# A two-layer decoder kernel: causal attention masked on its diagonal blocks, with a further contraction row for the masked blocks and buffers cleared one by one

## The reference, cut to what matters

```
scores = jnp.einsum('bhid,bhjd->bhij', q, k) * scale
causal_mask = jnp.triu(jnp.full((Ll, Ll), -10000.0, dtype=scores.dtype), 1)
attn = jax.nn.softmax(scores + causal_mask, axis=-1)
y_softmax = jnp.einsum('bhij,bhjd->bhid', attn, v)
```

## Time and profile before

| | us |
|---|---|
| median of 3 runs | 6885.89 |
| lowest and highest | 6875.44, 6894.77 |
| the profiled execution, its own time | 6882.64 |
| its span, first to last instruction | 6880.8 |
| TensorE's mean granted clock over the span | 0.874 of full speed |
| PE, PEld, DVE, ACT, POOL busy | 5450.3, 2943.8, 4755.6, 3102.1, 2124.6 |

### The profile page before, as it was taken

How to read it: one execution, slowest core, us unless ns; L and a number is a source line. 1 busy time by engine, 2 the same in 40 slices (tenths; PEclk the granted TensorE clock), 3 DMA queues, 4 the chain that set the end, 5 groups by cost and what they waited for, 6 DMA issues and landing times. The chain is left out here.

```text
span 6880.8 us, 138736 instructions
## 1 busy us (share of the span) xinstructions
PE 5450.3 (79%) x46679; PEld 2943.8 (43%) x46679; DVE 4755.6 (69%) x8810; ACT 3102.1 (45%) x4684; POOL 2124.6 (31%) x2727
## 2 busy tenths in 40 slices
PE   3686657688888846978498999996567799999659
PEld 2343335222222223434356888885535233333234
DVE  5464675899999954456656777763555899999644
ACT  0233434477777722224433444442224577777512
POOL 0100325577777730004026555541306000000000
PEclk6898978799999978989796888886778899999879
DMA  2220007222222210002243443431108222222100
GB/s 63 47 45 16 6 14 258 68 58 58 59 59 59 57 32 20 0 0 106 103 143 113 115 119 114 121 98 63 56 16 270 62 64 64 65 65 64 53 12 12
DMA packets 747524, 484.29 MB, mean 70 GB/s; under 512 B 516504, under 2 KB 682240, under 8 KB 741568
## 3 DMA queue, kind: packets, MB, share of 16 engines
q1 hardware_dynamic: 747200, 480.04, 24.5%
HBM read 282.34 MB, written 196.37 MB: 70 GB/s over the span
## 5 line engine op out<-in xcount | busy, mean ns | idle before, releaser
L1504 ACT ACTIVATE c0a_raised<-c0a_sb 128x1024 f32<-128x1024 f32 (+1 forms) x832 | 836.3, 1025 | 317.3 <-PE c0a_sb L1316 313.0
L1269 POOL TENSOR_SCALAR c0a_prob<-c0a_raised 128x1024 f32<-128x1024 f32 (+1 forms) x832 | 864.7, 1039 | 366.7 <-ACT c0a_raised L1504 335.7
L1504 ACT ACTIVATE c1a_prob<-c1a_sb 128x1024 f32<-128x1024 f32 (+1 forms) x832 | 828.5, 1029 | 206.6 <-PE c1a_sb L1316 202.9
L1392 DVE TENSOR_REDUCE c1a_pmax<-c1a_sa 128x2 f32<-128x802 f32 (+1 forms) x704 | 698.2, 992 | 68.2 <-PE c1a_sa L1284 64.2
L1392 DVE TENSOR_REDUCE c0a_pmax<-c0a_sa 128x2 f32<-128x802 f32 (+1 forms) x704 | 697.1, 990 | 55.2 <-PE c0a_sa L1284 51.1
L1284 PE MATMUL c0a_sa<-c0a_K,c0a_Q 48*128 48x401 bf16 (+1 forms) x2048 | 471.8, 349 | 181.7 <-DVE c0a_pmax L1392 107.7
L1284 PE MATMUL c1a_sa<-c1a_K,c1a_Q 48*128 48x401 bf16 (+1 forms) x2048 | 466.2, 346 | 103.9 <-DVE c1a_pmax L1392 49.1
L1335 PE MATMUL c0a_pv<-c0a_prob,c0a_V 128*9 128x256 f32 x6656 | 524.9, 386 | 4.7 <-POOL c0a_prob L1269 4.1
L1335 PE MATMUL c1a_pv<-c1a_prob,c1a_V 128*9 128x256 f32 x6656 | 519.4, 383 | 0.7 <-issue 0.5
L1284 PEld LDWEIGHTS c0a_sa<-c0a_K,c0a_Q 48*128 48x128 bf16 x2048 | 129.1, 93 | 667.7 <-DVE c0a_pmax L1392 340.4
L3020 PE MATMUL dd_lb<-dd_src 64*128 64x128 f32 (+1 forms) x3584 | 357.2, 345 | 38.9 <-DVE dd_AB L3211 15.7
(11 more groups left out here) (606 smaller groups left out, 11199.4 us busy)
## 6 DMA issues: line engine op xcount, KB each, us to landing
dd_src<-unit_in SPq DMA_DIRECT2D x32, 1024.0 KB, 7.8
k_ctx<-c0k_parts SPq DMA_DIRECT2D x16, 1200.8 KB, 6.1
c0a_K<-k_ctx SPq DMA_DIRECT2D x128, 150.1 KB
k_ctx<-c1k_parts SPq DMA_DIRECT2D x16, 1200.8 KB, 5.9
c1a_K<-k_ctx SPq DMA_DIRECT2D x128, 150.1 KB
unit_in<-ds_raw SPq DMA_DIRECT2D x32, 512.0 KB, 2.6
unit_v<-ds_vs SPq DMA_DIRECT2D x32, 512.0 KB, 2.6
unit_in<-dp_res SPq DMA_DIRECT2D x32, 512.0 KB, 2.9
```

Of the source, the lines that this page charges most:

```text
L1269: pool.tensor_scalar(prob[0:r, in_ring(v, c), :, :, :], raised[0:r, in_ring(v, c), :, :, :], 1.0, math.exp(-FLOOR), ALU.min, ALU.max).then ...
L1392: dve.tensor_reduce(pmax[:, u, :, 2 * pr + s, k], sa2[:, :, 0:w], AX.X, ALU.max).then_inc(a_reduced, 1)
L1504: act.activation(dst[0:r, in_ring(v, c), :, :, :], sb_[0:r, in_both(v, c), :, :, :], ACT.Exp).then_inc(b_exp, 1)
```

## The change

It touches four things in `attention_stage`:

- The mask of pass A is now one triangle `above` of 128 x 128, read twice, and written to quarters 0 and 3 of the piece (256 columns instead of 512). The mask of pass B is one triangle `below`, again read twice by each of its two matmuls, and written only to the 128 queries on the diagonal of the key tile (256 columns instead of 512).
- The block that is masked whole gets its -10000 from contraction row 64 (`FULL`): `K` holds 125 there for keys 128 to 255, `Q` holds -80 for queries 0 to 127. `K` is zero instead of one in rows 0 to 95.
- DVE clears and fills the buffers of `K` and row 64 of `Q`, POOL clears those of `Q`, each one buffer at a time, and a load waits for its own buffer alone. `V` is not cleared any more.
- PE's first piece waits for all fills of DVE (`K_set`, `Q_set`) and for six steps of the masks, which POOL now makes ahead of `VG`. The stage has three semaphores more.

```diff
-            maskA = st.sb("maskA", [P, 2, L], BF16)
-            maskB = st.sb("maskB", [P, 2, L], BF16)
+            above = st.sb("above", [P, P], BF16)
+            below = st.sb("below", [P, P], BF16)
...
             @block.sync
             def _(sp):
-                sp.wait_ge(zeroed, 3)
...
-                    if not early(n, LOADS):
+                    if early(n, LOADS):
+                        sp.wait_ge(K_zeroed, v + 1)
+                        sp.wait_ge(Q_zeroed, v + 1)
+                    else:
                         sp.wait_ge(b_used, (n - LOADS + 1) * NC)
                         sp.wait_ge(VG_ready, n - LOADS + 1)
...
             @block.gpsimd
             def _(pool):
-                pool.memset(K[:, :, :, :], 1.0).then_inc(zeroed, 1)
-                pool.memset(Q[:, :, :, :], 0.0).then_inc(zeroed, 1)
-                pool.memset(V[:, :, :, :, :], 0.0).then_inc(zeroed, 1)
+                for v in range(LOADS):
+                    pool.memset(Q[:, v, :, :], 0.0).then_inc(Q_zeroed, 1)
+                pool.memset(scaled[:, :], 0.0).then_inc(masks_ready, 1)
+                pool.memset(above[:, :], 0.0).then_inc(masks_ready, 1)
+                pool.memset(below[:, :], 0.0).then_inc(masks_ready, 1)
...
                     if causal:
-                        pe.matmul(sa[:, i % 2, :], scaled[:, :], maskA[:, :, :].rearrange("p s t -> p (s t)"),
+                        quarters = sa[:, i % 2, :].rearrange("p (q t) -> p q t", t=P)
+                        pe.matmul(quarters[:, 0:4:3, :], scaled[:, :], above[:, :].unsqueeze(1).to_broadcast([P, 2, P]),
                                   start=True, stop=False, skip_group_check=True)
...
                     if causal:
                         for x in range(2):
-                            pe.matmul(sb_[:, c0(u, c), 2 * x:2 * x + 2, :], scaled[:, :],
-                                      maskB[:, t, :].unsqueeze(1).to_broadcast([P, 2, L]),
+                            pe.matmul(sb_[:, c0(u, c), 2 * x:2 * x + 2, t * P:(t + 1) * P], scaled[:, :],
+                                      below[:, :].unsqueeze(1).to_broadcast([P, 2, P]),
                                       start=True, stop=False, skip_group_check=True)
...
-                pe.wait_ge(zeroed, 3)
-                if causal or clip:
-                    pe.wait_ge(masks_ready, 8 if causal else 3)
+                pe.wait_ge(masks_ready, 6)
+                pe.wait_ge(K_set, 2 * LOADS)
+                pe.wait_ge(Q_set, LOADS)
...
+                for v in range(LOADS):
+                    dve.memset(K[0:MROW, v, :, :], 0.0).then_inc(K_zeroed, 1)
+                    dve.memset(K[MROW:KR, v, :, :], 1.0).then_inc(K_set, 1)
+                    dve.wait_ge(K_zeroed, v + 1)
+                    dve.memset(K[FULL:FULL + 1, v, :, P:L], BIG_B).then_inc(K_set, 1)
+                    dve.wait_ge(Q_zeroed, v + 1)
+                    dve.memset(Q[FULL:FULL + 1, v, :, 0:P], BIG_A).then_inc(Q_set, 1)
                 for i in range(NA):
                     a_reduce(0, 0, i)
```

More of the change, by code:

```diff
@@ L610, in attention_stage @@
     PAIRS = [(0, 0), (1, 0), (2, 0), (0, 1), (1, 1), (0, 2)]
+    FULL = 64
     MROW = 96
@@ L662, in attention_stage @@
         V_loaded = [st.sem(f"V_loaded{v}") for v in range(LOADS)]
-        zeroed = st.sem("zeroed")
+        K_zeroed = st.sem("K_zeroed")
+        Q_zeroed = st.sem("Q_zeroed")
+        K_set = st.sem("K_set")
+        Q_set = st.sem("Q_set")
         ones_set = st.sem("ones_set")
@@ L802, in _ @@
             def _(pool):
-                pool.memset(K[:, :, :, :], 1.0).then_inc(zeroed, 1)
-                pool.memset(Q[:, :, :, :], 0.0).then_inc(zeroed, 1)
-                pool.memset(V[:, :, :, :, :], 0.0).then_inc(zeroed, 1)
+                for v in range(LOADS):
[3 more added lines that the diff above has]
+                pool.memset(below[:, :], 0.0).then_inc(masks_ready, 1)
+                pool.wait_ge(masks_ready, 3)
+                pool.affine_select(out=scaled[:, :], in_=scaled[:, :], compare_op=ALU.not_equal, fill=BIG_A,
+                                   base=0, pattern=[[-1, P]], channel_multiplier=1).then_inc(masks_ready, 1)
+                pool.affine_select(out=above[:, :], in_=above[:, :], compare_op=ALU.is_ge, fill=BIG_B,
+                                   base=0, pattern=[[-1, P]], channel_multiplier=1).then_inc(masks_ready, 1)
+                pool.affine_select(out=below[:, :], in_=below[:, :], compare_op=ALU.is_ge, fill=BIG_B,
+                                   base=0, pattern=[[1, P]], channel_multiplier=-1).then_inc(masks_ready, 1)
                 pool.memset(VG[:, :, :, :, :, :], 0.0).then_inc(ones_set, 1)
@@ L808, in _ @@
                 pool.memset(VG[:, :, :, :, :, HD:HD + 1], 1.0).then_inc(ones_set, 1)
[L809 to L821, removed]
                 if clip:
```

## The result

| | changed | before |
|---|---|---|
| device time, median (us) | 6849.05 (6837.62 to 6860.53, 4 runs) | 6880.78 (6875.44 to 6894.77, 4 runs) |
| ratio to before, 95% interval | 0.9945 [0.993, 0.996] | |
| profiled execution, its time / its span | 6860.53 / 6858.8 | 6882.64 / 6880.8 |
| granted PE clock, mean | 0.870 | 0.874 |

The changed kernel is faster by 31.7 us, 0.55%.

What follows compares the result with a forecast made beforehand. PE and DVE, waiting for each other's pieces, and the maxima chain were taken to bound a unit. +0.7 - 1.0 - 4.5 - 40.5 - 1.3 = -46.6 us against 6882.64 gave 6836.0, stated as 6838; range 6824 to 6852.

Steps and rivals of the forecast that it cites:

- start of the stage to the first piece: Stage start: the early load gains nothing because PE's first piece waits for all DVE fills, until 212.1; +0.7 us.
- first piece to the last split: First unit's 16 pieces go at DVE's pace, so smaller masks give little; first scores have fewer columns: -1.0 us.
- last split to the first scores: First maxima: their small DMAs no longer stand behind late loads, the queue being empty at 226; -4.5 us, otherwise 0.
- from there to the next stage, 15 x 2.7 + 1.3: Units: smaller masks save 2.7 us in each of fifteen, 40.5 us, and 1.3 us in the last unit's six chunks.
- The choice of 1.047 ns for an element: DVE's start fills: pace taken from its other rows, not the fills' 0.833 ns, so they end at 212.1.
- The rival of the fast fills: Stage start: DVE's fills go at the pace of their own rows, 8.9 us less, 6829; chance 0.13.
- The rival that the two hinder each other: Stage start: POOL's and DVE's clearing block each other, DVE up to 13.75 us later, 6852; chance 0.06.
- DVE would pace the first half: A unit's first half: DVE's 11.6 us of work sets the pace; 12.7 us taken, from 14.96.
- The second rival: Units: the handover between PE and DVE eats more, 18 us back, 6856; chance 0.12.
- nothing happens in the units: Units: the chain through reductions and maxima sets the pace, only -5 us from the start, 6878; chance 0.07.
- The slower rival: Units: PE's clock falls to 1.2 GHz, 10.8 us more a unit, slower from 5 of 15 on; chance 0.04.

Runs made afterwards that it cites:

- early_start: Changed kernel with DVE filling only K's zeros and buffer 0's constant rows, POOL filling those of buffers 1 to 3 later: 6823.72 us, ratio 0.9916.
- big_masks: Changed kernel with both masks 512 columns wide again, clearing still one by one: 6879.79 us, ratio 0.9997 to the kernel before.
- big_A: Changed kernel with the mask of pass A alone back at 512 columns: 6881.61 us, one run.
- big_fourth: Changed kernel with both masks 512 columns wide again and each chunk's fourth piece ahead of the scores: 6861.01 us, one run.
- both_gap: Changed kernel with early_start's fills, fourth piece ahead of the scores, POOL's rows for buffers 2 and 3 held until the first maxima are split: 6806.98 us.
- load_late: both_gap with the load of buffer 2 issued after the first maxima DMAs instead of ahead of them: 6806.58 us, ratio 0.9884 to the kernel before.
- no_masks: Changed kernel without the mask matmuls of both passes, diagonal blocks left unmasked: 6806.03 us, one run.
- again: The changed kernel once more with no edit: 6838.49 us, ratio 0.9934 to the kernel before.
- big_B: Changed kernel with the mask of pass B alone back at 512 columns: 6875.48 us, one run.

## Why the prediction was right

The forecast was right in sign, size and place. Its sum was -46.6 us; the stage shows -41.9. That 6838 lies within a microsecond of the second median is luck: the sum was 4.7 us too large, and the clock in `dp` differs by as much between two executions of one kernel. By its steps, from the profiled executions:

| step | forecast | measured |
|---|---|---|
| start of the stage to the first piece | +0.7 | 44.33 - 43.30 = +1.0 |
| first piece to the last split | -1.0 | 15.78 - 15.03 = +0.75 |
| last split to the first scores | -4.5 | 2.09 - 6.57 = -4.5 |
| from there to the next stage, 15 x 2.7 + 1.3 | -41.8 | 336.4 - 375.6 = -39.2 |
| other stages | 0 | +19.8, nearly all the clock in `dp` |

*The fills.* The choice of 1.047 ns for an element was right in its result and wrong in its reading, so the hit is luck. The rows of the fills say 1.76 us for 2048 elements and 3.47 for 4096, 0.85 ns an element, near rows 7. But each is followed by 0.38 to 0.91 us of "issue", and the rounds take 11.02 us, as the slower figure gave (by it DVE ended at 212.1; the first piece stands at 212.13). The rival of the fast fills took the rows' own durations and left out what stands between them. By the Trainium skill's one cycle an element (VectorE: DVE Perf Modes, "Zero memsets can be issued as uint32"; 0.96 GHz by the same page's "Specifications") the round would take 10.7 us, an estimate. The trace agrees with it for the round, within 0.35 us, and not for the single fill: the next one starts 3.95 us behind the start of the fill of 4096 elements, for which the same estimate is 4.27 us.

*Clearing side by side.* POOL's four fills take 13.87 us beside DVE's, where one of the two whole fills took 13.75 alone, and DVE's rounds take 11.02 us with POOL busy and without. The rival that the two hinder each other is refuted for fills. `early_start` shows that it isn't so for a cast of DVE beside a fill of POOL. There the rows agree with the Trainium skill (SBUF — State Buffer, "SBUF: two separate sides"), by which an instruction of GpSimd, or one of DVE in a two-port mode, holds the ports that the two share until it ends, and the other is blocked fully: 3.22 and 1.57 us, to the end of each fill. That these casts run in such a mode is inferred; no row shows the mode.

*The first pieces.* Here the sign was wrong: +0.75 instead of -1.0. I had said DVE's pace (0.70 us a piece) would hold. These are the windows of the 16 pieces, first of the changed kernel, then of before:

```profile
212.13:227.91 15.78, 12.06 (x49) 4.74 (x49) 12.32 (x23) 0.00 (x0) 0.00 (x0) 0.50 0.01 1
```

```profile
211.47:226.50 15.03, 11.15 (x49) 3.92 (x49) 12.15 (x23) 1.70 (x2) 0.00 (x0) 0.84 0.35 82
```

PE has less to do and stays busy longer, since its clock stays at 1.2 GHz over all sixteen; before it had risen on the way. The other runs tell which part of the change this belongs to. The clock rose 3.6 to 5.4 us behind the first piece in the four kernels with the wide mask in pass A (before, `big_masks`, `big_A`, `big_fourth`), and in none of the eight others before the last split. `big_A` differs from the changed kernel in that mask alone. These are the second 5 us from the first piece, first of the changed kernel, then of `big_A`:

```profile
217.13:222.13 5.00, 4.56 (x20) 1.82 (x19) 4.17 (x7) 0.00 (x0) 0.00 (x0) 0.50 0.00 0
```

```profile
217.31:222.31 5.00, 4.40 (x24) 1.51 (x22) 4.53 (x8) 0.00 (x0) 0.00 (x0) 0.97 0.00 0
```

So the smaller mask of pass A took the higher clock from the first pieces: from the first piece to the last split `big_A`, with more columns, needs 15.45 us and the changed kernel 15.78. The prediction had no term for it.

*The maxima.* Without a load just ahead in the queue the step is what was forecast, and `both_gap` and `load_late` show the cause from the other side: with a load just ahead of the DMAs it is 5.6 us, without it 2.1.

*The units.* The mechanism was right, the first half is 12.87 us where 12.7 was forecast, the chain stays (5.75). The unit of 20.84 us is followed by longer ones, and the mean is 21.10 and 20.94 us in two executions: 2.44 to 2.60 saved in place of 2.7. In the first a single unit took 23.45 us (see *The clock*); without it the mean is 20.92. In reading rows 2 the prediction took the single wait of 11.0 us for one of the hand-over. The reasoning that DVE would pace the first half was too sharp, as `no_masks` shows: a microsecond off PE is worth 0.68 whatever the width. The second rival (21.5 us and more) is refuted; `big_masks` refutes that nothing happens in the units.

*The clock.* The slower rival put the loss into the units. Its sign appeared once in the changed kernel, behind the maxima DMAs of 331.56, from which 23.45 us pass to the next ones:

```profile
334.17:335.68 1.51, 0.00 (x1) 0.01 (x1) 0.00 (x0) 0.00 (x0) 0.00 (x0) 1.00 0.13 22
336.10:339.60 3.50, 3.50 (x22) 1.85 (x21) 0.86 (x3) 1.05 (x2) 0.00 (x0) 0.51 0.07 10
```

PE stood idle for 1.51 us, waiting for the maxima DMAs, and ran at 1.2 GHz soon after. That unit is 2.5 us longer than the others, far from the 54 us that the rival needed. `big_fourth` and `no_masks` have two such stretches each, `load_late` one, `again` none. The clock took more time, 20 us, in a stage that I had not looked at, because nothing is changed there. `again` shows this loss to vary from execution to execution; that the change has a part in it isn't excluded. The four longest stretches are those of the changed kernel (twice), `big_masks` and `big_A`; `big_B`, which shares as much with them, has 20.5 us. It stays open.

*The range.* 6824 to 6852 was reckoned from 6836, with the 3 us for the runs at the upper end only; from 6838 and with them at both ends it is 6823 to 6854. Nothing hangs on the difference.

## What to carry to other kernels

Where two engines pass small buffers to each other, work taken off one comes back in part (here 0.68 of PE's), and the order of the pieces can be worth as much as their size: one piece moved ahead of the scores gave 1.1 to 1.3 us of a unit for no less work. Where two waits end close together, taking away one shows little (0.55 us here) until the other is gone too (3.4 us more). Taking columns off PE's first pieces also left its clock at the lower level for longer here, so a part of the gain went back. A buffer that is cleared for its own load only helps if nothing else that the first use waits for is cleared behind it in a row: here the load had landed 25 us before PE began. A small DMA on the path wants no large load ahead of it in the queue, but a load moved behind it must still be issued before the next small one is ready.

## What the runs showed of the hardware

- A fill on DVE of 2048 elements in a partition takes 1.76 us in its row, whether of bf16 or of uint32, one of 4096 takes 3.47, and 0.38 to 0.91 us pass to the next one. The row alone understates the pace by about a fifth.
- Fills of DVE and of POOL into SBUF run side by side without loss (13.87 against 13.75 us; 11.02 us both ways), but a 32x128 cast of DVE beside a POOL fill took 3.22 us in place of 0.21, until the fill had ended; a subtraction of the same size beside the same fill took its usual 0.28.
- In the `dp` stage the granted clock was 0.50 for 17 to 65 us in the same work, from PE's idle time ahead of its first matmul on; of it PE worked some 9 us before the clock rose in the kernel before and some 51 us in the changed one. The stage took 196 to 219 us with it. The stretch differed by 10 us between two executions of one kernel.
- In the units the granted clock fell to 0.50 for 3 to 4 us behind idle times of PE of 1.51 us (changed kernel), 1.93 and 1.88 (`big_fourth`) and 4.56 (`load_late`).
